# One VectorE instruction per head for the leaky step and the maximum over keys of a graph attention layer

## The reference

```python
h = jnp.einsum('bnd,ade->bane', feat_in, W)
th = jnp.tanh(h)
attn_src = jnp.einsum('bane,aeo->bano', th, w_src)
attn_dst = jnp.einsum('bane,aeo->bano', th, w_dst)
attn = attn_src + jnp.swapaxes(attn_dst, 2, 3)
attn = jnp.where(attn >= 0, attn, LEAKY_ALPHA * attn)
attn = jnp.where(mask, jnp.float32(-999.0), attn)
attn = jax.nn.softmax(attn, axis=-1)
feat_out = jnp.einsum('banm,bame->bane', attn, h) + b
```

## Time and profile before

| | us |
|---|---|
| median of 3 runs | 1120.95 |
| lowest and highest run | 1120.76, 1123.92 |
| profiled execution, first to last instruction | 1121.2 |
| VectorE, leaky step L1129, 64 instructions | 111.9 |
| VectorE, maxima L1136, 64 instructions | 111.6 |
| ScalarE, copy L793, 64 instructions | 93.2 |

### The profile page before, as it was taken

How to read it: one execution, slowest core, us unless ns; L and a number is a source line. 1 busy time by engine, 2 the same in 40 slices (tenths; PEclk the granted TensorE clock), 3 DMA queues, 4 the chain that set the end, 5 groups by cost and what they waited for, 6 DMA issues and landing times.

```text
span 1121.2 us, 32794 instructions
## 1 busy us (share of the span) xinstructions
PE 1047.1 (93%) x10890; PEld 950.8 (85%) x10890; DVE 1025.2 (91%) x2138; ACT 893.5 (80%) x1739; POOL 947.2 (84%) x781
## 2 busy tenths in 40 slices
PE   4899999999999999999999999999999999999761
PEld 4888889889898988889898888889888888988641
DVE  5589999999999999999999999999999999999854
ACT  4568888888888888888888888888888888888753
POOL 2158889988888998888899888889988888998775
PEclk9899999999999999999999999999999999999975
DMA  6103333232333333234333323433332243332232
GB/s 200 32 21 73 98 84 89 76 86 66 82 97 83 89 79 84 70 79 97 83 89 81 82 74 74 97 83 89 83 82 77 69 97 83 93 81 72 47 67 73
DMA packets 188717, 91.33 MB, mean 81 GB/s; under 512 B 158864, under 2 KB 183696, under 8 KB 188688
## 3 DMA queue, kind: packets, MB, share of 16 engines
q1 hardware_dynamic: 188688, 90.95, 32.7%
HBM read 31.61 MB, written 12.58 MB: 39 GB/s over the span
## 4 chain that ended last, share of the span: by engine, by line
PE 73%; issue 9%; DVE 8%; POOL 4%; ACT 3%; DMA 1%; DVEq 0%; SPq 0%; POOLq 0%; ACTq 0%
PE lin L459 42%; PE zp L554 6%; PE zp L613 3%; PE zp L617 3%; PE fp L583 3%; PE tp L498 3%; PE tp L567 3%; PE tp L626 2%; DVE sd L1008 2%; PE tp L595 2%; PE fp L586 2%; PE fp L640 2%; ACT th L736 1%; ACT sd_t L765 1%; POOL z L1353 1%
## 5 line engine op out<-in xcount | busy, mean ns | idle before, releaser
L1353 POOL TENSOR_TENSOR z<-z,z_max 128x1536 f32<-128x1536 f32 x64 | 176.4, 2757 | 21.3 <-DVE z_max L1136 18.9
L818 ACT ACTIVATE z<-z,log_scale 128x1536 f32<-128x1536 f32 x64 | 101.3, 1583 | 53.7 <-POOL z L1353 53.6
L1360 POOL TENSOR_TENSOR p_lo<-z,p_hi 128x1024 f16<-128x1024 f32 x64 | 137.3, 2145 | 2.3 <-ACT p_hi L824 2.3
L1365 POOL TENSOR_TENSOR f<-f,x_kept 128x384 f32<-128x384 f32 x64 | 65.0, 1016 | 72.0 <-DVE f L1168 72.0
L1318 POOL TENSOR_TENSOR prod<-th,w_sd_rows 128x768 f32<-128x768 f32 x64 | 117.9, 1842 | 6.6 <-ACT th L736 6.4
L784 ACT ACTIVATE p<-p,p_min 128x128 f32<-128x128 f32 x384 | 118.9, 399 | 4.7 <-DVE p_min L1068 4.7
L1129 DVE SCALAR_TENSOR_TENSOR z<-zp,z 128x1536 f32<-128x1536 f32 x64 | 111.9, 1748 | 2.3 <-ACT z L793 2.3
L1136 DVE TENSOR_REDUCE z_max<-z 128x12 f32<-128x1536 f32 x64 | 111.6, 1744 | 0.1
L793 ACT ACTIVATE z<-zp 128x1536 f32<-128x1536 f32 x64 | 93.2, 1457 | 17.8 <-PE zp L617 17.8
L1331 POOL TENSOR_TENSOR v_part<-v_res,v_part 128x384 bf16<-128x384 f32 x64 | 63.0, 984 | 35.8 <-ACT v_part L755 33.8
L459 PE MATMUL lin<-xt_hi,Wq_hi 128*128 128x256 f32 x288 | 81.0, 281 | 12.7 <-DVE Wk_lo L926 12.4
(11 more groups left out here) (162 smaller groups left out, 4394.2 us busy)
## 6 DMA issues: line engine op xcount, KB each, us to landing
xt_raw<-x_t SPq DMA_DIRECT2D x32, 384.0 KB, 4.0
x_raw<-x SPq DMA_DIRECT2D x32, 384.0 KB, 3.2
x_kept<-x SPq DMA_DIRECT2D x64, 192.0 KB, 2.3
out<-out_tile SPq DMA_DIRECT2D x64, 192.0 KB, 1.9
adj<-adj SPq DMA_DIRECT2D x64, 32.0 KB, 1.9
dst_row<-sd_t SPq DMA_DIRECT2D x64, 9.0 KB
p1t_hi<-p_hi SPq DMA_TRANSPOSE x64, 3.2
p1t_lo<-p_lo SPq DMA_TRANSPOSE x64, 3.1
```

Of the source, the lines that this page charges most:

```text
L818: act.activation(z[:, g, :], z[:, g, :], ACT.Exp, bias=log_scale[:, :]).then_inc(z_exp[g].sem, 1)
L1353: pool.tensor_tensor(zs, zs, z_max[:, g, :].unsqueeze(2).to_broadcast([128, H1, N]), ALU.subtract)\
L1360: pool.tensor_tensor(p1_lo[:, g, :], z[:, g, PE_HEADS * N:], p1_hi[:, g, :], ALU.subtract).then_inc(w1_lo[g].sem, 1)
```

## The change

ScalarE's copy becomes `z_raise`: it writes 4·relu(zp) into `z`. VectorE's `z_leak` and `z_maxima` become one step `z_leak_max`, 12 instructions, one per head on 128 columns. Each writes 0.2·(zp + z), which is max(zp, 0.2 zp), and also gives the maximum of what it writes, from -3e38 on, into a column of `z_max`. The semaphores `z_copied` and `z_maxed` go; `z_leaky` is now raised by the last of the 12, and both TensorE's `zp` and GpSimd's `z_subtract` wait for it. In VectorE's order `z_leak_max` stands where `z_leak` stood.

```diff
-                def z_copy(g):
+                def z_raise(g):
                     act.wait_ge(z_mm[g].sem, now(z_mm[g]))
 
                     act.wait_ge(w1_lo[g].sem, prev(w1_lo[g]))
                     act.wait_ge(wt_mm[g].sem, now(wt_mm[g]))
-                    act.activation(z[:, g, :], zp[:, :, :].rearrange("p b n -> p (b n)"), ACT.Copy)\
-                        .then_inc(z_copied[g].sem, 1)
+                    act.activation(z[:, g, :], zp[:, :, :].rearrange("p b n -> p (b n)"), ACT.Relu, scale=4.0)\
+                        .then_inc(z_raised[g].sem, 1)
...
-                def z_leak(g):
-                    dve.wait_ge(z_copied[g].sem, now(z_copied[g]))
-                    dve.scalar_tensor_tensor(out=z[:, g, :], in0=zp[:, :, :].rearrange("p b n -> p (b n)"), scalar=0.2,
-                                             in1=z[:, g, :], op0=ALU.mult, op1=ALU.max).then_inc(z_leaky[g].sem, 1)
-
-                def z_maxima(g):
-                    dve.wait_ge(z_leaky[g].sem, now(z_leaky[g]))
+                def z_leak_max(g):
+
+                    dve.wait_ge(z_raised[g].sem, now(z_raised[g]))
 
                     dve.wait_ge(z_sub[g].sem, prev(z_sub[g]))
-                    dve.tensor_reduce(z_max[:, g, :], z[:, g, :].rearrange("p (a n) -> p a n", a=H1),
-                                      AX.X, ALU.max).then_inc(z_maxed[g].sem, 1)
+                    turn.apart()
+                    for h in range(H1):
+                        last = dve.tensor_tensor_reduce(out=z[:, g, N * h:N * (h + 1)],
+                                                        in0=zp[:, h // 4, N * (h % 4):N * (h % 4 + 1)],
+                                                        in1=z[:, g, N * h:N * (h + 1)], scale=0.2, scalar=-FAR,
+                                                        op0=ALU.add, op1=ALU.max, accum_out=z_max[:, g, h:h + 1])
+                    last.then_inc(z_leaky[g].sem, 1)
...
-                turn.late(1, z_leak, 0)
+                turn.late(1, z_leak_max, 0)
                 turn.step(0, value_residue, 0)
                 turn.late(0, add_residual, 0)
-                turn.late(1, z_maxima, 0)
                 turn.late(0, context_low, 1)
                 turn.late(0, stats0, 0)
                 turn.late(0, moments0, 0)
                 turn.late(1, gate_raised, 1)
-                turn.late(1, z_leak, 1)
+                turn.late(1, z_leak_max, 1)
                 turn.late(0, add_residual, 1)
                 turn.late(0, variance0, 0)
-                turn.late(1, z_maxima, 1)
...
-                    pool.wait_ge(z_maxed[g].sem, now(z_maxed[g]))
+                    pool.wait_ge(z_leaky[g].sem, now(z_leaky[g]))
```

More of the change, by code:

```diff
@@ L25 @@
 MASKED = 9e15
+FAR = 3.0e38
 HALF_TOP = 57344.0
@@ L305, in two_layer_graph_attention @@
         dst_flat = [signal(f"dst_flat{g}", 1, DONE_BY_DMA) for g in range(2)]
-        z_mm, z_maxed = pair_of("z_mm", 1), pair_of("z_maxed", 1)
-        z_copied, z_leaky = pair_of("z_copied", 1), pair_of("z_leaky", 1)
+        z_mm = pair_of("z_mm", 1)
+        z_raised, z_leaky = pair_of("z_raised", 1), pair_of("z_leaky", 1)
         z_sub, z_exp = pair_of("z_sub", 1), pair_of("z_exp", 1)
@@ L855, in body @@
                 turn.late(0, context_high, 0)
-                turn.late(1, z_copy, 0)
+                turn.late(1, z_raise, 0)
                 turn.step(0, value_part1, 0)
@@ L860, in body @@
                 turn.step(0, value_part2, 0)
-                turn.late(1, z_copy, 1)
+                turn.late(1, z_raise, 1)
                 turn.late(1, gate_tanh, 0)
```

## The result

The changed kernel takes 1150.05 us (median of 4 runs, 1149.86 to 1150.84), the kernel before, with a fourth run, 1122.32 us (1120.76 to 1123.92): ratio 1.0247, 95% interval 1.023 to 1.0264. It is slower by 28 us; 1177 were predicted, in a range from 1148 to 1240. The measured time lies 2 us above the lower end of that range. The profiled execution has a span of 1148.5 us against 1121.2. A span is not a time: this execution's time is 1150.2 us, 1.7 above its span, and in every run listed here the time lies 1.7 to 3.6 us above the span.

What follows compares the result with a forecast made beforehand. TensorE was taken as the bound, VectorE right behind. Two stalls, 0.99 + 0.81 = 1.80 us a turn, gave 54.0 us in 30 turns, 56 us with the remaining pairs: 1121.2 + 56 = 1177 us, range 1148 to 1240.

Steps and rivals of the forecast that it cites:

- Z: VectorE's time per graph from the first new instruction's start to the next instruction's start: 3.12 us, bounds 2.7 to 4.08.
- What bounds the kernel: TensorE is the bound, idle 0.46 us a turn, with VectorE right behind it, idle 1.19 us.
- ScalarE's relu: ScalarE's relu in place of the 1457 ns copy from PSUM: zero change, bounds plus and minus 0.02 us.
- VectorE's work: Per graph two long instructions, 3.32 us, give way to 12 times two, 3.12 us; VectorE gets back 0.40 us per turn.
- First stall: TensorE's scores of graph 1 wait for `zp`, released after all 24 instructions: 0.99 us a turn.
- Second stall: TensorE's third chunk of queries and keys waits for the `lin` bank, held until graph 1's late residual: 0.81 us a turn.
- The sum: Both stalls together, 1.80 us a turn or 2 Z - 4.44, in 30 turns 54.0 us; 56 us with the remaining pairs.
- The cover: TensorE's gate rows of graph 1 need `y` of graph 0, which was forecast to come 0.14 us early.
- A: Rival: VectorE's saving of 0.40 us per turn shortens the run by 12 us, to 1108 us; chance 0.05.
- B: Rival: only the first stall remains, 32 us, giving 1153 us; chance 0.06.
- C: Rival: VectorE's instruction with a maximum runs at half rate, 0.40 us per head, giving 1283 us; chance 0.08.
- D: Rival: Z about 2.2, so the stalls nearly vanish and nothing is gained, 1121 us; chance 0.03.

Runs made afterwards that it cites:

- the leaky step by heads: The kernel before with its leaky step cut into 12 instructions of 128 columns, copy and maximum kept: 1165.49 us, ratio 1.0383.
- Bank by bank: The changed kernel with a semaphore for each `zp` bank of four heads, for graph 1's scores: 1140.35 us, ratio 1.0155.

## Why the prediction was right, step by step

The mechanism was right: both late releases are there, at the places and with the releasers forecast, and each goes when it is mended. The sizes were not: the loss is half of what was forecast, and the time lies in the range only by the room that was added below 1151, the lower end that the working gave. The one term that carries this is Z.

**What bounds the kernel.** TensorE, as forecast: taking 1.4 us a turn off VectorE does not shorten the turn. But VectorE's 1.19 us of idle time are no slack, as the leaky step by heads showed.

**ScalarE's relu.** Zero was right: 1455 ns against 1457.

**VectorE's work: the mis-sized term.** Z was put at 3.12 us per graph and is 2.57, below the lower bound of 2.7; a head's 0.21 us lie below the 0.225 that the prediction itself had named as a sign of being wrong, so the price of the new instructions was wrong by its own test. Of the 0.26 us per head, the 0.20 for the 128 columns was right (0.21 with accumulator, 0.198 without), and the 0.06 for the accumulator's read was wrong: accumulator and read add some 0.01. Its price was taken from L1117, an instruction of one column with inputs of its own; the read runs beside the start of the next head.

The Trainium skill (Vector Engine (DVE) Microarchitecture Reference, section "Measured stream behaviour on trn2") gives 1.04 ns per column and about 75 ns per instruction. That fits the main instruction (0.208 us, an estimate, against 0.21 in the trace). The trace does not agree for the read, for which the estimate had another 0.076.

**First stall.** Forecast 0.99 us, measured 0.61; place and releaser are as forecast. With Z = 2.57 the forecast's own working gives 0.44. Another 0.15 is a term that was missing: the first head starts 575.83 - 574.16 = 1.67 us after ScalarE's relu starts, where the leaky step started 563.08 - 561.56 = 1.52 us after the copy.

**Second stall.** Forecast 0.81 us, measured 0.27; with Z = 2.57 the working gives 0.26. That this fits so closely is partly luck: the hand-over of the bank takes 0.15 us (585.20 to 585.35), not the 0.06 read off the drain, and small differences the other way, such as graph 1's 2.53 us in place of 2.57, make up for it.

**The sum.** 2 Z - 4.44 gives 0.70 us for Z = 2.57; with the late start of 0.15 that is 0.85, against 0.93 measured; a part of the 0.10 us at VectorE's pair makes up the rest. The forecast's 34.4 us for a turn came out as 33.58. Against the span of 1148.5 the forecast's 1177 was 29 us too much: the mis-sized Z, 2 × 0.55 us in each of 30 turns, is 33 us of it, and the lag that was left out takes 5 back.

**The cover.** The 0.14 us over the wait for `y` of graph 0 held in the changed kernel. Bank by bank, with the stall ahead of it gone, the same wait cost 0.24 us.

**The rivals.** A (VectorE's saving counts) falls: with nothing released late any more the time is 1123.62, not 1108. B (one stall) falls, although its 1153 us lie near the measured time: both stalls are there, each smaller, and each was taken away (the second but for 0.08 us) by itself. A time alone does not choose between mechanisms. C (half rate) falls: 0.21 us per head, not 0.40. D (nothing measurable) falls by the time.

## What to carry to other kernels

A fused step that raises its semaphore at its end hands back all its operands only there. Before fusing, ask which of them somebody waits for and how much slack that release has: here 0.46 us, against 0.9 us by which the fused step took longer to give `zp` back and 0.15 by which it started later; and a lighter engine made the kernel slower. Fused work can be handed back in pieces, and a step that others want can go between the pieces; but each mended release uncovers the next one a few tenths of a microsecond behind it.

The Trainium skill (Perfetto Trace Analysis, section "Matmuls") advises rotating groups of matmuls through PSUM banks, so that the emptying of one overlaps the next group. The runs agree in that overlap: with `zp` handed back bank by bank TensorE's next masks start while VectorE still empties the third bank, and the wait ahead of graph 1's masks went from 0.61 us to nothing.

## What the runs showed of the hardware that was not expected

- The read of a running maximum costs next to nothing behind a 128-column instruction: it is 83 ns long, and two heads stand 0.21 us apart with it and 0.198 without.
- The first of the new instructions starts 0.22 us after the end of the relu it waits for; the long instruction in its place started 0.07 us after the copy, and the first of twelve plain short ones 0.06. The cause is open.
- An instruction that waits for the semaphore of the one ahead of it on VectorE starts 1.78 us after the start of a 1536-column step, one that does not wait for it 1.66.
- VectorE loses 0.10 us once a turn, in every kernel here with the new instructions, at a place that moved when six semaphore increments were added earlier in its list.
